# An attention sandwich on one core: the attention result is packed channel-major through DRAM instead of transposed on TensorE, and the first and last turns get lists of their own

## The chip, the cores and the metric

One core of one Trainium2 chip. The metric is the time of one execution on the device in microseconds. Inputs are float32, and every matrix product is held close to float32 accuracy: each operand is split into a high and a low part in a reduced float32 format (`..._hi`, `..._lo`), and three products (hi·hi, hi·lo, lo·hi) are added.

## What is computed

The input x has 32 batches of 512 tokens with 256 channels. The mask lets a block of 128 tokens see itself and every block whose number is a multiple of 24; with four blocks that is block 0.

```python
allowed = (bi[:, None] == bi[None, :]) | is_global[:, None] | is_global[None, :]   # bi: block of a token
def attn(x):                       # 16 heads of 16 channels
    q, k, v = split(x @ w_qkv.T + b_qkv)
    scores = einsum('bhqd,bhkd->bhqk', q / 4, k) + mask
    return einsum('bhqk,bhkd->bhqd', softmax(scores), v) ... @ w_out.T + b_out
def ffn(h):
    return relu(h @ W1 + b1) @ W2 + b2           # 256 -> 1024 -> 256
x = x + layernorm(attn(layernorm(x)))
x = x + layernorm(ffn(layernorm(x)))
```

## The kernel before

**Jobs and lists.** The work of a batch is cut into jobs, and each of the five instruction streams (TensorE, ScalarE, VectorE, GpSimd, and SP, which issues nearly all DMAs) has a list `ORDER[engine]` of jobs for one turn of the loop. A job is (name, number, batch offset); turn i does it for batch i + offset, so the stages of up to six batches overlap. An engine works through its list strictly in order, and waits by semaphore where a job needs another engine's result. In the first and last turns the same lists run, with the jobs of batches that do not exist left out (`steps`, `there`). TensorE's stream is unrolled over all turns; the others loop.

**The jobs of one batch.** `load_xa`, `ln1_stats/mean/rstd/apply` (normalization, in halves), `x1` (16 transposes on TensorE), `x1_hi`/`x1_lo` (ScalarE and VectorE read the accumulators), `qk` 0 to 3 and `v` 0, 1 (products), `qk_hi`/`qk_lo`, and `load_stack` 0 to 7: six DMAs each that stack the parts of q and k of two heads in the tile `stack`. `scores_max` 0 to 19 compute scores once, `reduce` takes row maxima from the accumulators, `max_t`, `copy_max`, `store_row`, `load_row` bring the negated maxima as one more row into `stack`; `scores` 0 to 19 compute the scores again with the maximum subtracted, `exp` writes `probs`. `pv` n multiplies the probabilities of four heads by `values`, in which each head has its 16 channels and a column of ones, so that row 16 of each head's 32 result rows is the denominator. After this:

- `read_o` n (ScalarE, L535): accumulator to `o_t`, 128 rows (4 heads x 32) by 512 tokens.
- `o_t` n (TensorE, L452 to L454): eight small transposes to token-major. Four a batch.
- `normal_o` n (VectorE, L643 to L657): reciprocal of the denominators, two multiplications into `o_n`.
- `o2` (TensorE, L449 to L451): 16 transposes of `o_n` back to channel-major; `o2_hi`, `o2_lo` (L543, L625) read the accumulators.
- `op` 0, 1: output projection; `op_out`, `lny_*`, `x1_add` (residual), `x1_keep`, `ln2_*`, `x2` (transposes), `x2_hi/lo`, `f1` 0 to 7, `relu`, `h_lo` (GpSimd), `f2` 0 to 3, `f2_out`, `lnf_*`, `final_add`, `store`.

**Accumulators.** There are four pairs of banks (`RING`). The fourth entry of a TensorE job names its pair; the job before it on that pair must have been read out first (`unit_before`, `free`).

**Loading the weights.** SP loads all weights at the start; ScalarE writes their high parts and VectorE their low parts, `w_qkv` first, the rest after `qk` 1 of batch 0 (`split_first`, `split_rest`). GpSimd's memsets of `stack` and `values` (`set_ones`) follow `ln1_rstd` 1 of batch 0.

Of the kernel before, what the change touches and what calls it, by code (L numbers as in the profile page):

```python
# [20 lines left out]

ORDER = {
    "PE": [
        ("scores_max", 17, -2, 1), ("qk", 1, -1, 2), ("scores", 6, -2, 0), ("pv", 0, -2, 3),
        ("scores", 7, -2, 0), ("f1", 4, -4, 2), ("scores", 8, -2, 3), ("f1", 6, -4, 1), ("scores", 9, -2, 0),
        ("f1", 5, -4, 2), ("o_t", 0, -2, 3), ("scores_max", 18, -2, 0), ("f1", 7, -4, 1),
        ("scores_max", 19, -2, 3), ("qk", 2, -1, 0), ("max_t", 3, -2, 3), ("scores_max", 0, -1, 2),
        ("qk", 3, -1, 0), ("scores", 10, -2, 3), ("scores_max", 1, -1, 2), ("pv", 1, -2, 1),
        ("scores", 11, -2, 3), ("scores_max", 2, -1, 2), ("scores", 12, -2, 1), ("o_t", 1, -2, 0),
        ("scores_max", 3, -1, 3), ("scores", 13, -2, 2), ("scores_max", 4, -1, 1), ("f2", 2, -4, 0),  # L30
        ("scores_max", 5, -1, 3), ("scores", 14, -2, 2), ("scores", 15, -2, 1), ("f2", 3, -4, 0),
        ("scores", 16, -2, 2), ("pv", 2, -2, 3), ("max_t", 0, -1, 1), ("scores", 17, -2, 0),
        ("scores_max", 6, -1, 2), ("scores", 18, -2, 3), ("o_t", 2, -2, 1), ("scores", 19, -2, 0),
        ("scores_max", 7, -1, 2), ("scores_max", 8, -1, 1), ("scores_max", 9, -1, 3), ("pv", 3, -2, 0),
        ("scores", 0, -1, 2), ("v", 0, -1, 1), ("x2", 0, -3, 3), ("o_t", 3, -2, 0), ("scores", 1, -1, 2),
        ("v", 1, -1, 1), ("o2", 0, -2, 0), ("scores", 2, -1, 2), ("f1", 0, -3, 3), ("scores_max", 10, -1, 1),
        ("f1", 2, -3, 2), ("f1", 1, -3, 3), ("scores_max", 11, -1, 0), ("f1", 3, -3, 2),
        ("scores_max", 12, -1, 1), ("op", 0, -2, 0), ("max_t", 1, -1, 3), ("scores_max", 13, -1, 1),
        ("scores_max", 14, -1, 3), ("op", 1, -2, 0), ("x1", 0, 0, 1), ("scores", 3, -1, 2), ("f2", 0, -3, 3),
        ("scores", 4, -1, 2), ("scores_max", 15, -1, 0), ("scores_max", 16, -1, 1), ("f2", 1, -3, 3),  # L40
        ("qk", 0, 0, 2), ("scores", 5, -1, 0), ("max_t", 2, -1, 3),
    ],
    "ACT": [
# [753 lines left out]
```

## Time and profile before

| | |
|---|---|
| three runs | 2062.49, 2060.56, 2061.07 us; median 2061.07 |
| the profiled execution | 2061.84 us, of it 2060.0 from the first to the last instruction |
| TensorE busy | 1938.2 us, 94% |
| VectorE / ScalarE / GpSimd busy | 1536.7 / 1408.6 / 722.8 us |
| DMA | 160.61 MB, 132817 packets, mean 78 GB/s |
| mean granted TensorE clock | 0.977 |

Busy time is the time in which at least one instruction of the engine runs. The matmuls overlap one another, so a group's own durations add up to more than it costs; the distance from one group's start to the next is what it costs. PE is TensorE, PEld its weight loads, DVE VectorE, ACT ScalarE, POOL GpSimd, SPq the issuing of DMAs by SP. L377 is line 377 of the kernel.

### The profile page before, as it was taken

The page shows a single profiled execution, that of the slowest core. Times are in us where ns is not written, and L with a number is a line of the kernel's source. Part 1 is how long each engine was busy: PE and PEld are TensorE (multiplying, and loading weights), DVE is VectorE, ACT ScalarE, POOL GpSimd, SP SyncE. Part 2 cuts the span into 40 slices and gives each one's busy share as a digit, 9 for nine tenths or more (in the row PEclk, how much of TensorE's full clock was granted, in tenths as well). Part 3 has the DMA queues.
Part 4 walks back from the last instruction along what each step waited for, and adds up shares of the span by engine and source line. Part 5 has one row for each costly group of instructions (what it writes and reads, how often), then busy time and mean ns, then how long its engine had stood idle before and what let it go on. Part 6 is the DMA issues. An engine that isn't in the chain of part 4 may idle for free. (4 is left out here: it accounts for less than half of the span.)

```text
span 2060.0 us, 70899 instructions
## 1 busy us (share of the span) xinstructions
PE 1938.2 (94%) x27904; PEld 1588.0 (77%) x27904; DVE 1536.7 (75%) x2916; ACT 1408.6 (68%) x2341; POOL 722.8 (35%) x905
## 2 busy tenths in 40 slices
PE   3879999999999999999999999999999999999985
PEld 2557887788888778888877888787788878778765
DVE  6577777777787777778777787877778787777631
ACT  2446677777777777777777776777777677777653
POOL 2013333333333333333333333333433334343343
PEclk8789999999999999999999999999999999999998
DMA  4343343334334333433433343343334334333200
GB/s 124 71 84 73 76 90 68 80 80 93 78 81 91 68 79 81 92 78 82 91 67 77 84 90 79 80 91 66 79 84 88 79 82 89 68 80 76 54 27 16
DMA packets 132817, 160.61 MB, mean 78 GB/s; under 512 B 29408, under 2 KB 82400, under 8 KB 132576
## 3 DMA queue, kind: packets, MB, share of 16 engines
q1 hardware_dynamic: 132048, 156.29, 35.8%
q8 instruction: 222, 3.64, 0.8%
q10 hardware_dynamic: 528, 0.52, 0.1%
q14 instruction: 19, 0.16, 0.0%
HBM read 38.21 MB, written 17.83 MB: 27 GB/s over the span
## 5 line engine op out<-in xcount | busy, mean ns | idle before, releaser
L613 DVE TENSOR_REDUCE max_bias<-p_pair 128x4 f32<-128x1024 f32 (+1 forms) x640 | 761.4, 1215 | 104.1 <-PE p_pair L363 87.9
L530 ACT ACTIVATE probs<-p_pair 128x1024 f32<-128x1024 f32 x640 | 638.8, 1027 | 246.4 <-PE p_pair L363 134.9
L746 POOL TENSOR_TENSOR h_lo<-h_f,h_hi 128x512 fp32r<-128x512 f32 x256 | 329.8, 1288 | 477.5 <-ACT h_hi L562 477.4
L366 PE MATMUL p_pair<-stack 49*128 49x256 f32 (+1 forms) x3072 | 352.3, 314 | 36.3 <-ACT probs L530 15.0
L562 ACT ACTIVATE h_f<-p_pair,b_s 128x256 f32<-128x256 f32 x512 | 247.9, 484 | 119.3 <-PE p_pair L393 119.3
L366 PEld LDWEIGHTS p_pair<-stack 49*128 49x128 f32 (+1 forms) x3072 | 241.3, 191 | 111.6 <-ACT probs L530 46.8
L393 PE MATMUL p_pair<-x_hi,w_hi 64*128 64x256 f32 (+1 forms) x2560 | 302.6, 308 | 13.0 <-DVE x_lo L625 5.5
L393 PE MATMUL p_pair<-w_hi,h_hi 64*128 64x256 f32 x2048 | 286.7, 277 | 10.0 <-POOL h_lo L746 7.4
L393 PE MATMUL p_pair<-x_hi,w_lo 64*128 64x256 f32 (+1 forms) x2560 | 295.9, 302 | 0.0
L393 PE MATMUL p_pair<-x_lo,w_hi 64*128 64x256 f32 (+1 forms) x2560 | 295.7, 302 | 0.0
L393 PE MATMUL p_pair<-w_lo,h_hi 64*128 64x256 f32 x2048 | 284.1, 274 | 0.0
L393 PE MATMUL p_pair<-w_hi,h_lo 64*128 64x256 f32 x2048 | 283.9, 274 | 0.0
L562 ACT ACTIVATE h_hi<-p_pair,b_s 128x256 fp32r<-128x256 f32 x512 | 249.1, 486 | 0.0
L363 PE MATMUL p_pair<-stack 49*128 49x512 f32 (+1 forms) x1024 | 220.2, 433 | 19.6 <-DMA stack<-qk 7.3
L393 PEld LDWEIGHTS p_pair<-x_hi,w_hi 64*128 64x128 f32 x2560 | 213.5, 187 | 24.1 <-DVE max_bias L613 13.0
L393 PEld LDWEIGHTS p_pair<-x_hi,w_lo 64*128 64x128 f32 x2560 | 215.8, 186 | 11.7
L393 PEld LDWEIGHTS p_pair<-x_lo,w_hi 64*128 64x128 f32 x2560 | 215.5, 186 | 11.7
L393 PEld LDWEIGHTS p_pair<-w_hi,h_hi 64*128 64x128 f32 x2048 | 192.9, 185 | 15.1 <-POOL h_lo L746 6.0
L432 PEld LDWEIGHTS p_pair<-probs,values 128*32 128x32 f32 x3072 | 106.3, 112 | 120.5 <-issue 81.0
L393 PEld LDWEIGHTS p_pair<-w_lo,h_hi 64*128 64x128 f32 x2048 | 193.1, 185 | 2.8
L432 PE MATMUL p_pair<-probs,values 128*32 128x256 f32 x3072 | 194.2, 385 | 0.0
L393 PEld LDWEIGHTS p_pair<-w_hi,h_lo 64*128 64x128 f32 x2048 | 192.7, 185 | 0.0
(77 smaller groups left out, 2815.6 us busy)
## 6 DMA issues: line engine op xcount, KB each, us to landing
stack<-qk SPq DMA_DIRECT2D x1536, 64.0 KB, 2.3
xr<-x SPq DMA_DIRECT2D x32, 512.0 KB, 4.0
out<-yf SPq DMA_DIRECT2D x64, 256.0 KB, 2.2
xa<-x SPq DMA_DIRECT2D x31, 512.0 KB, 4.5
shift_rows<-max_t SPq DMA_DIRECT2D x128, 8.0 KB, 1.3
stack<-shift_rows SPq DMA_DIRECT2D x128, 8.0 KB
probs<-w SPq DMA_DIRECT2D x2, 512.0 KB, 4.9
probs<-w_qkv_t SPq DMA_DIRECT2D x2, 384.0 KB, 5.2
```

Of the source, the lines that this page charges most:

```text
L363: last = nc.tensor.matmul(dst[:, j, :], stack[r, stationary, at, 0:P], stack[r, moving, at, :], start=True, stop=True)
L366: last = nc.tensor.matmul(dst[:, j, col:col + HALF].rearrange("p (a n) -> p a n", a=2), stack[r, stationary, at, kb * P:(kb + 1) * P], two ...
L393: last = nc.tensor.matmul(dst[:, u, cols], stationary(r), moving(r), start=part == 0 and at == 0 and m == 0, stop=part == 1 and m == adden ...
L432: last = nc.tensor.matmul(two(o, kb), v, probs[:, prob_slot(n, c), j, col:col + HALF] .rearrange("p (a n) -> p a n", a=2), start=False, st ...
L530: nc.scalar.activation(probs[:, prob_slot(quad, c), :, :], banks("scores", n)[:, :, :], ACT.Exp, scale=SCALE).then_inc(exp_done, 1)
L562: last = nc.scalar.activation(dst, banks("f1", n)[:, n % 2, u * HALF:(u + 1) * HALF], ACT.Relu, bias=b1_s[:, m:m + 1])
L613: nc.vector.tensor_reduce(dst, src, axis=AX.X, op=ALU.max, negate=True).then_inc(red_done, 1)
L746: nc.gpsimd.tensor_tensor(h_parts[1][:, m:m + 2, :], h_f[:, n % 2, :, :], h_parts[0][:, m:m + 2, :].bitcast(F32), ALU.subtract).then_inc(h ...
```

## The change

1. **No `o_t` and `o2` on TensorE.** `read_o` writes one of two halves of a bigger `o_t`. `store_o` (SP) issues two DMAs for each quad of heads: the four denominator rows spread over 128 partitions of `den_q`, and all 128 rows to `o_rows` in DRAM. `load_o` n brings, for eight heads, the 16 wanted rows of each back as `o_ch[:, n, :]`, 128 channels by 512 tokens, in the memory of `ya`.
2. **Reciprocals.** `inverse` n (VectorE, 128x32), `store_inv` n (to `inv_rows` in DRAM), `load_inv` n (one DMA that repeats each head's row for its 16 channels into `inv_b`). `normal_o` n multiplies `o_ch` by `inv_b`; `o2_hi` n and `o2_lo` n split the result. There are two of each a batch. `w_out` is permuted on the host to the new channel order.
3. **Lists.** `ORDER` is new for every engine; `FIRST` and `LAST` are explicit lists of the jobs before and after the full turns. There are 28 full turns on TensorE.
4. **Start.** Weights come on SP's and ScalarE's queues, each part with a semaphore of its own (`W_STAGE`); their splits are jobs in the lists, with low parts mostly on GpSimd. x of batch 0 comes in two halves. The first memset of `stack` runs at the very start, the second after `ln1_apply` of batch 0, that of `values` later.

```diff
                     wait(act, pv_mm, b, QUADS, n + 1)
-                    wait(act, mm["o_t"], b, QUADS, n)
-                    nc.scalar.activation(o_t[:, :], banks("pv", n)[:, 0, :], ACT.Copy).then_inc(ot_done, 1)
+                    for s in (den_in, o_out):
+                        wait(act, s[n % 2], b, 32, 16 * (n // 2))
+                    nc.scalar.activation(o_t[:, n % 2, :], banks("pv", n)[:, 0, :], ACT.Copy).then_inc(ot_done, 1)
...
+                elif what == "store_o":
+                    rows_free, den_free = count(sp, b, 16, 0), count(sp, b, KD, n // 2 + 1 - KD)
+                    wait(sp, ot_done, b, QUADS, n + 1)
+                    reached(sp, o_in[n // 2], rows_free)
+                    reached(sp, inv_done, den_free)
+                    heads = slice(4 * (n % 2), 4 * (n % 2) + 4)
+                    sp.dma_start(den_q[:, n // 2, n % 2, :],
+                                 o_t[HD:P:32, n % 2, :].rearrange("h (m t) -> h m t", t=DT)).then_inc(den_in[n % 2], 16)
+                    sp.dma_start(o_rows[n // 2, heads].rearrange("h c n -> (h c) n"),
+                                 o_t[:, n % 2, :]).then_inc(o_out[n % 2], 16)
+                elif what == "load_o":
...
+                    reached(sp, x1_done, added)
+                    sp.dma_start(o_ch[:, n, :], o_rows[n, :, 0:HD, :].rearrange("h c n -> c h n")).then_inc(o_in[n], 16)
+                elif what == "store_inv":
...
+                    sp.dma_start(inv_rows[n].rearrange("(j h) (m t) -> (h m) j t", j=2, t=DT),
+                                 inv_q[:, n, :, :]).then_inc(inv_out[n], 16)
+                elif what == "load_inv":
...
+                    sp.dma_start(inv_b[:, n, :],
+                                 inv_rows[n].unsqueeze(0).broadcast_to([HD, H // 2, L])).then_inc(inv_in[n], 16)
...
-                    wait(pe, ev["o_t"], b, QUADS, QUADS)
-                    last = transposed(dst, lambda r, m: o_n[r, m % KB, m // KB * P:(m // KB + 1) * P], KD * KB)
-                elif what == "o_t":
-                    wait(pe, ot_done, b, QUADS, n + 1)
-                    last = transposed(dst, lambda r, m: o_t[r, m * P:(m + 1) * P], KB)
...
+                elif what == "inverse":
+                    for j in range(2):
+                        wait(dve, den_in[j], b, 32, 16 * (n + 1))
+                    wait(dve, inv_out[n], b, 16, 0)
+                    nc.vector.reciprocal(inv_q[:, n, :, :], den_q[:, n, :, :]).then_inc(inv_done, 1)
                 elif what == "normal_o":
+                    wait(dve, inv_in[n], b, 16, 16)
+                    wait(dve, o_in[n], b, 16, 16)
+                    nc.vector.tensor_tensor(o_ch[:, n, :], o_ch[:, n, :], inv_b[:, n, :], ALU.mult).then_inc(on_done, 1)
```

A part of TensorE's new list, from the last `pv` of a batch to its `op` one turn of the loop later (offsets are against the turn):

```python
("pv", 3, -2, 0), ("scores_max", 12, -1, 1), ("scores", 0, -1, 3), ("max_t", 1, -1, 0), ("v", 0, -1, 2),
("x2", 0, -3, 3), ("x1", 0, 0, 0), ("scores", 1, -1, 1), ("v", 1, -1, 2), ("scores", 2, -1, 1),
("f1", 0, -3, 3), ("f1", 2, -3, 1), ("f1", 1, -3, 3), ("scores_max", 13, -1, 2), ("qk", 0, 0, 0),
("f1", 3, -3, 1), ("scores", 3, -1, 2), ("qk", 1, 0, 0), ("op", 0, -2, 3), ...
```

and of VectorE's, and SP's, for the same stretch:

```python
("x2_lo", 0, -4), ("inverse", 1, -3), ("v_out", 0, -2), ("normal_o", 0, -3), ("x1_lo", 0, -1),
("reduce", 13, -2), ("normal_o", 1, -3), ("o2_lo", 0, -3), ("o2_lo", 1, -3), ("qk_lo", 0, -1), ...
("store_o", 3, -3), ("load_xr", 0, -3), ("store_row", 1, -2), ("store_inv", 1, -3), ("load_xa", 0, 0),
("load_o", 1, -3), ("load_inv", 1, -3), ("load_stack", 6, -2), ...
```

## Rows read from the trace of the kernel before

**Rows 1.** Engine totals of the page: busy us (share of the span) xinstructions.
```profile
PE 1938.2 (94%) x27904; PEld 1588.0 (77%) x27904; DVE 1536.7 (75%) x2916; ACT 1408.6 (68%) x2341; POOL 722.8 (35%) x905
```

**Rows 2.** Windows: from:to, length; busy us PE, PEld, DVE, ACT, POOL; PEclk, DMA, GB/s.
```profile
1001.55:1061.67 60.12, 59.15 (x876) 48.93 (x872) 47.55 (x91) 43.73 (x74) 22.32 (x28) 1.00 0.38 82
0.00:178.00 178.00, 123.89 (x1202) 86.90 (x1204) 120.66 (x184) 72.80 (x91) 23.66 (x37) 0.81 0.40 89
178.00:1915.00 1737.00, 1705.55 (x25134) 1408.48 (x25136) 1369.12 (x2621) 1262.76 (x2106) 643.47 (x807) 1.00 0.38 81
1915.00:2060.00 145.00, 108.77 (x1575) 92.59 (x1572) 46.90 (x113) 73.05 (x147) 55.66 (x62) 0.90 0.11 31
```

**Rows 3.** Timeline of VectorE, `values`: start us, length us, engine, line, operation.
```profile
289.29 1.21 DVE L638 TENSOR_TENSOR values<-p_pair,max_bias 128x1024 f32<-128x1024 f32 x1
...
1855.52 1.21 DVE L638 TENSOR_TENSOR values<-p_pair,max_bias 128x1024 f32<-128x1024 f32 x1
```

**Rows 4.** Timeline of TensorE about the transposes of one batch.
```profile
1007.30 0.40 PE L393 MATMUL p_pair<-w_hi,x_hi 64*128 64x256 f32 x4
...
1008.72 0.66 PE L377 MATMUL p_pair<-ident,xr 64*128 64x64 f32 x16
1009.21 0.42 PE L377 MATMUL p_pair<-ident,o_t 64*128 64x64 f32 x8
1009.43 0.48 PE L363 MATMUL p_pair<-stack 49*128 49x512 f32 x2
...
1011.17 0.66 PE L377 MATMUL p_pair<-ident,o_n 64*128 64x64 f32 x16
1011.63 0.49 PE L366 MATMUL p_pair<-stack 49*128 49x256 f32 x4
```

**Rows 5.** Waits of TensorE, 200 to 1900 us: us in total, times, longest.
```profile
PE p_pair L366 <- DVE o_n L652: 5.1, 28, 0.2
```

**Rows 6.** Groups by line: busy us, mean ns of one | idle before.
```profile
L652 DVE TENSOR_TENSOR o_n<-p_pair,den 128x128 f32<-128x128 f32 x256 | 62.4, 285 | 4.4
L668 DVE TENSOR_TENSOR yf<-p_pair,b_s 128x512 f32<-128x512 f32 x64 | 43.9, 687 | 65.0 <-PE p_pair L393 49.4 <-DMA out<-yf 15.6
L625 DVE TENSOR_TENSOR o_lo<-p_pair,o_hi 128x1024 fp32r<-128x1024 f32 x32 | 38.9, 1214 | 0.8 <-ACT o_hi L543 0.8
```

**Rows 7.** Timeline of GpSimd and VectorE; line 695: ns shortest, median, longest.
```profile
1044.00 1.29 POOL L746 TENSOR_TENSOR h_lo<-h_f,h_hi 128x512 fp32r<-128x512 f32 x1 [0.17 <-ACT h_hi L562]
1044.08 1.23 DVE L695 SCALAR_TENSOR_TENSOR nmr_lny<-mv_lny,rstd_lny 128x2 f32<-128x2 f32 x1
...
L695 DVE SCALAR_TENSOR_TENSOR nmr_lny<-mv_lny,rstd_lny x64: 130/146/1271, 130.1 to 1996.8; 128x2 f32<-128x2 f32 x64
```

**Rows 8.** DMA issues of the page: count, KB each, median us to landing.
```profile
out<-yf SPq DMA_DIRECT2D x64, 256.0 KB, 2.2
xa<-x SPq DMA_DIRECT2D x31, 512.0 KB, 4.5
shift_rows<-max_t SPq DMA_DIRECT2D x128, 8.0 KB, 1.3
```

**Rows 9.** Timeline of SP's issuing of DMAs.
```profile
1001.86 0.33 SPq L332 DMA_DIRECT2D shift_rows<-max_t  x1
1004.88 0.54 SPq L336 DMA_DIRECT2D stack<-shift_rows  x1
...
1046.72 3.80 SPq L323 DMA_DIRECT2D stack<-qk  x6
```

**Rows 10.** Timeline of the start: VectorE, GpSimd, TensorE.
```profile
8.44 7.28 DVE L705 TENSOR_SCALAR xa<-xa,mv_ln,rstd_ln 128x256 f32<-128x256 f32 x2 [0.26 <-POOL rstd_ln L739]
8.47 7.10 POOL L726 MEMSET stack<- 32x4096 f32 x2
33.48 0.80 PE L363 MATMUL p_pair<-stack 48*128 48x512 f32 x2 [6.62 <-DMA stack<-qk]
```

More of the change, by code:

```diff
@@ L29 @@
[L29 to L39, printed above, removed]
@@ L89 @@
+READ = {"scores_max": 20, "scores": 20, "max_t": 4, "pv": 4, "op": 1, "x2": 1, "f1": 8, "f2": 2,
         "x1": 1, "qk": 4, "v": 1}
 PAIR_OF = {job[:2]: job[3] for job in ORDER["PE"]}
[L91 to L94 removed]
 def sandwich(nc, x, w_qkv_t, b_qk, b_v, w_out_t, b_out, w1, b1, w2, b2, ident_in, out):
@@ L228, in opens, with full_turns @@
             return what not in CROSSED or which % 2 == 0
-        def unit_before(what, which, i):
-            jobs = [job for job in ORDER["PE"] if opens(*job[:2])]
-            mine = [job[:2] for job in jobs].index((what, which))
-            for at in range(mine - 1, -4 * len(jobs), -1):
-                name, n, off, pair = jobs[at % len(jobs)]
-                b = i + at // len(jobs) + off
-                if pair == PAIR_OF[what, which] and there(b):
-                    return name, n, b
-            return None
+        def full_turns(engine):
+            offsets = [job[2] for job in ORDER[engine]]
+            return TURNS[0] - min(offsets), NB - max(offsets) - TURNS[1]
@@ L241, in reads, with steps @@
         def reads(name, n):
             return (n // 2 + 1) * READ[name] // PRODUCTS[name] if name in CROSSED else n + 1
-        def steps(eng, jobs, job, early=None, unrolled=False):
-            def turn(i):
-                todo = [(what, n, i + off) for what, n, off, *_ in jobs if there(i + off)]
+        def steps(eng, engine, job, early=None):
+            start, stop = full_turns(engine)
+            for what, n, b in FIRST[engine]:
+                job(what, n, b)
+            for what, n, off in ORDER[engine]:
+                job(what, n, start + off)
+            with eng.Fori(start + 1, stop) as i:
+                todo = [(what, n, i + off) for what, n, off in ORDER[engine]]
@@ L251, in turn @@
                 for at, (what, n, b) in enumerate(todo):
-                    if early and not isinstance(i, int):
+                    if early:
                         early(what, todo[at + 1:])
-                    job(what, n, b, i)
-            if unrolled:
-                for i in range(-AHEAD, NB + BEHIND):
-                    turn(i)
-                return
-            for i in range(-AHEAD, LOOP_FROM):
-                turn(i)
-            with eng.Fori(LOOP_FROM, NB - AHEAD) as i:
-                turn(i)
@@ L264, in steps @@
-            for i in range(NB - AHEAD, NB + BEHIND):
-                turn(i)
+                    job(what, n, b)
+            for what, n, b in LAST[engine]:
+                job(what, n, NB + b)
         def two(ap, kb):
```

537 lines of the change are left out of this document (391 added, 146 removed), and 12 rows, old and new, of tables (FIRST, LAST, ORDER).

## The prediction

> **What bounds the kernel now.** I read the engine totals first: TensorE is busy 1938.2 us of 2060.0, far more than VectorE at 75% or ScalarE at 68% [rows 1]. Then the windows [rows 2]: one turn of the loop (60.12 us) has TensorE busy for 59.15 us at full granted clock, VectorE for 47.55, ScalarE for 43.73. So a steady turn is TensorE's own work plus about 1 us of gaps. Next the length of a turn: the addition that writes `values` runs once for each batch, at 289.29 us for one and at 1855.52 us 26 batches later [rows 3], so 60.24 us a turn on average. Last, the ends. Between 178 and 1915 us lie 28.8 turns with 1705.55 us busy, 59.15 a turn. Thirty-two turns' work at that rate is 1893 us, so the other 167 us of the span are the idle time (54.1 us before 178 us, 31.5 in the middle, 36.2 after 1915 us [rows 2]) and about 45 us of slow clock (0.81 before 178 us, 0.90 after 1915 us). Those two ends are 90 us idle; the loop is nearly full.
>
> **The change, part by part**, against the profiled execution (2061.84 us, 2060.0 of it the span; the median of the runs shown is 2061.07, 0.8 lower, which I take off at the end).
>
> *Transposes removed from TensorE.* One `o_t` unit starts at 1009.21 us and the next unit at 1009.43: 0.22 us. The `o2` unit starts at 1011.17 us and its follower at 1011.63: 0.46 us [rows 4]. A batch has four and one: 4 x 0.22 + 0.46 = 1.34 us, all on the engine that bounds. 32 x 1.34 = **-43 us**. These steps are pipelined and I take starts, not durations, since durations overlap.
>
> *Waits that go with them.* An accumulator pair holding `o_t` is given free by `normal_o` on VectorE. In the steady part 28 turns wait there for 5.1 us in all [rows 5]. With five of 65 units gone from the ring, these go: **-5 us**. The rest of the gaps (mainly on `exp`) I leave as they are. Bounds: nothing, or as much again.
>
> *VectorE.* Out: eight multiplications of 285 ns and one `o2_lo` of 1214 ns, 3.5 us. In: two `normal_o` and two `o2_lo` on 128x512, each taken as the 687 ns of the 128x512 addition, 2.7 us [rows 6]. Four small reciprocals against two of twice the size I take as equal. So about 0.8 us less of 47.55. ScalarE: `o2_hi` becomes two of 128x512 instead of one of 128x1024, which by VectorE's 2 x 0.69 against 1.21 is at most +0.3 us of 43.73. Both are covered by 12 us or more of idle time a turn, so they cost nothing, and nothing is gained.
>
> *The two new SBUF-to-SBUF operations.* `normal_o` and `o2_lo` read two SBUF tensors, where before one input was an accumulator. The 128x2 `nmr_lny` of 1044.08 us lasts 1.23 us against a median of 146 ns, and GpSimd's `h_lo` runs from 1044.00 to 1045.29 beside it [rows 7]. So such an operation may be held by up to one `h_lo`, 1.1 us. In the new lists ScalarE issues `relu` 0 and 1 around the two `o2_hi`, so `h_lo` will run just when `normal_o` and `o2_lo` do. On VectorE that is at most 4 x 1.1 = 4.4 us a turn of 12 idle, no cost by itself; it counts in the chain below. (The Trainium skill, SBUF — State Buffer, section SBUF: two separate sides, says that an operation of VectorE with two SBUF inputs and a GpSimd operation that reads SBUF exclude each other for the whole instruction. The trace agrees, by the row of 1.23 us; by this rule the change would carry a delay that the removed form, with an accumulator as input, did not have.)
>
> *The round trip through DRAM.* After `pv` 3 the chain to `op` of that batch is: `read_o` (128x512, taken as 0.7 us like the addition of that size [rows 6]), `store_o` (denominators), `inverse`, `store_inv`, `load_inv` (queued behind `load_xa` and `load_o`), `normal_o` 1, `o2_hi`, `o2_lo` 1. Three transfers: the 8 KB store of the row maxima lands after a median of 1.3 us, but the load that waits for it once started 3.0 us after it (1001.86, 1004.88); loads from DRAM of 512 KB take 4.5 us, the 256 KB store 2.2 [rows 8, 9]. Low end, with the reciprocal as one of the 285 ns multiplications: 0.7 + 1.3 + 0.3 + 1.3 + 2.2 + 0.7 + 0.6 + 0.7 and 0.8 for eight handovers = 8.6 us. High end: 1.8 (behind one `lnf_apply`) + 3.0 + 0.3 + 3.0 + 4.5 + 0.7 + 0.6 + 0.7 + 0.8, plus two holds of 1.1 and about 2 us of queueing on VectorE and SP = 19.6 us. I take 13.9: small transfers of 2.0, the broadcast at 3, one hold and 2 us of queueing.
> The cover: between `pv` 3 and `op` 0 in the new TensorE list stand `v` twice and `f1` four times (24 matmuls of 256 columns each; `v` takes 1007.30 to 1008.72, 1.42 us), `qk` twice (half as many of 512 columns, so about the same), `x2` and `x1` (0.49, 1008.72 to 1009.21), six score units at about 0.3 and a `max_t` of 0.1 [rows 4]. 8 x 1.42 + 2 x 0.49 + 6 x 0.3 + 0.1 = 14.2 us. So the trip is covered by a hair: +0.2 us a turn x 28 = **+6 us**, from 0 to (19.6 - 14.2) x 28 = 151. If it is late, `op` on TensorE waits, and behind it the whole in-order list. VectorE waits too, at `inverse` 1 and `normal_o`: behind them stand `v_out`, `x1_lo` and `reduce` 13, whose results TensorE needs only for `scores_max` 13 and `qk` 0, later in the turn.
>
> *SP's queue.* Six stack copies are issued in 3.80 us, 0.63 each; other DMAs take from 0.33 us [rows 8, 9]. Before: 48 x 0.63 + 12 x 0.45 (between 0.33 and 0.54) = 36 us of a turn. Added: eight DMAs of `store_o` and six of the others, 14 at 0.33 to 0.63, 5 to 9 us. SP is then busy 41 to 45 us of 59: covered, unless its in-order waits (each new DMA has one) delay a stack copy. `load_stack` 4 of the next batch may go after `scores` 14, and `scores_max` 10 then needs it some 14 units and 8 to 9 us on; it takes 3.8 + 2.3 = 6.1 us. I count it at nothing, bound +1 us a turn. *Bytes.* 82 GB/s x 60.12 us is 4.9 MB a turn at 0.38 of the DMA engines [rows 2]; 2.1 MB are added (four stores and four loads of 256 KB), so about 0.55. Cover, nothing.
>
> *First turns.* Today VectorE's second `ln1_apply` lasts 7.28 us beside GpSimd's two memsets of 7.10 us at 8.44 us, and the first matmul waits for it [rows 10]. The new list does one memset before x has landed, and the other after `ln1` is applied: -6.5 us. `qk` 2 and 3 now run while the first stack copies are on their way (TensorE waits for these until 33.48 us [rows 10]): up to -2.6 us. From 58 to 178 us TensorE is idle another 20 us; own orders may win half: -10. Together **-18 us**, bounds -7 (the memset alone) and -35.
>
> *Last turns.* 36.2 us idle after 1915 us [rows 2]. The new list puts `f1` and `f2` of batch 30 (4 x 1.42 + 2 x 2.8 = 11 us) between the last `pv` and the last `op`, which covers most of the new trip; the same chain from `op` over two normalizations to `f1` stays. **-5 us**, bounds -15 and +8.
>
> Sum: -43 - 5 + 6 - 18 - 5 = **-65 us**, 2061.84 - 65 = 1996.8, and 0.8 less against the median: **1996 us**. The turn would be 60.24 - 1.34 - 0.2 + 0.2 = 58.9 us.
>
> **Rivals.**
> *A. The trip is late each turn by 1 to 2 us.* For it: the high end above, and the new hold by `h_lo`. Against it: I found 13.9 against 14.2. Price 1.2 x 28 = +34 us: about 2030.
> *B. Slower than before.* The same wait, larger: TensorE stops in front of `op` every turn until the broadcast reciprocals have landed. To cancel 65 + 6 us it must cost 71 / 28 = 2.5 us a turn, that is a trip of 16.7 us. Part of it could be the clock: it is 1.00 (2.4 GHz) in the full middle and falls to a mean of 0.81 and 0.90 at the ends, where TensorE has gaps [rows 2]. With a trip of 18 us, 3.8 us a turn: 1990 + 106 = 2096. For it: three serial DMAs on one queue that carries 40% more bytes. Against it: the middle values reach only 13.9.
> *C. SP is the late one.* Its waits push stack copies past their use: bound +1 us a turn, 2024.
> *D. More than forecast.* All gaps of TensorE but half go (31.5 us in the middle, -14 more) and the first turns give 25: about 1970.
> *E. It does not do what it says*: the units are gone, but TensorE's freed time turns fully into waits for `exp` and `reduce`, and only the first turns gain. VectorE and ScalarE are idle 12 and 16 us a turn, which speaks against it; 2061 - 5, within 0.2%.
>
> **How the numbers follow.** Forecast (1980 to 2012) 0.54, A 0.17, C 0.06, D 0.10, E 0.03, B 0.10. The range leaves out B and the far part of D: 1970 to 2045. A measurement of this kernel can tell about 0.2% from no change. Faster by more than that (under 2057): forecast, A, C, D = 0.87; the same 0.03; slower 0.10.
>
> **What would show it.** A turn of 58.9 us between two `values` additions; TensorE's busy time of 57.8 a turn; its 1536 transposes of `o_t` and `o_n` gone; no wait of TensorE's `op` matmuls on `o2_lo` over 0.5 us (A and B: 1.2 to 4 us there); first `scores_max` at about 25 us; SP's issues 41 to 45 us a turn; DMA share near 0.55. Wrong would be: a turn over 60 us; VectorE waiting at `normal_o` for a DMA for longer than its idle time; a granted clock under 1.00 in the middle.

## The result and the profile after

The changed kernel takes 2124.58 us (median; 2119.76 to 2132.95) against 2060.82 us for the kernel before: ratio 1.031, 95% interval 1.029 to 1.034. It is 64 us slower, where I had forecast 65 us faster. In all that follows a ratio is to runs of the kernel before on the same chip. The profiled execution took 2119.76 us, with a span of 2117.9 us.

The page's engine totals of the changed kernel (busy us, share of the span, instructions) answer to [rows 1]:

```profile
PE 1926.8 (91%) x26368; PEld 1568.7 (74%) x26368; DVE 1545.5 (73%) x2689; ACT 1407.5 (66%) x2375; POOL 751.4 (35%) x910
```

The 1536 transposes are gone (27904 - 26368), yet TensorE's busy time fell by only 11 us. Windows of the changed kernel, one full turn and the middle, in the columns of [rows 2]:

```profile
1035.28:1096.85 61.57, 58.26 (x828) 47.91 (x826) 48.71 (x86) 43.70 (x74) 23.01 (x28) 1.00 0.49 114
300.00:1800.00 1500.00, 1417.94 (x19930) 1165.30 (x19932) 1163.12 (x2026) 1055.95 (x1790) 553.93 (x674) 0.99 0.49 113
```

and the same middle of the kernel before:

```profile
300.00:1800.00 1500.00, 1472.79 (x21712) 1216.51 (x21708) 1183.94 (x2271) 1087.83 (x1811) 554.34 (x698) 1.00 0.39 81
```

In a turn TensorE is busy 58.26 us (forecast 57.8, before 59.15), but the turn is 61.57 us (forecast 58.9). Idle time in the middle went from 27 to 82 us of 1500, and the mean granted clock fell below 1.00, which I had named as a sign of being wrong. The `values` additions of batches 4 and 30 give the average turn, as in [rows 3]:

```profile
290.12 1.16 DVE L906 TENSOR_TENSOR values<-p_pair,max_bias 128x1024 f32<-128x1024 f32 x1
...
1904.97 1.23 DVE L906 TENSOR_TENSOR values<-p_pair,max_bias 128x1024 f32<-128x1024 f32 x1
```

(1904.97 - 290.12) / 26 = 62.11 us against 60.24. What TensorE waited for in the middle: first the changed kernel, then the one before (each row: who waited, for whom, us in total, times, longest):

```profile
PE p_pair L658 <- DVE o_lo L884: 41.4, 25, 2.0
PE p_pair L631 <- DVE max_bias L876: 17.4, 48, 0.6
PE p_pair L631 <- ACT probs L796: 9.9, 24, 0.4
PE p_pair L628 <- ACT probs L796: 4.2, 23, 0.2
```

The kernel before:

```profile
PE p_pair L366 <- ACT probs L530: 8.0, 50, 0.2
PE p_pair L366 <- DVE o_n L652: 4.5, 25, 0.2
PE p_pair L366 <- DVE max_t L617: 4.2, 24, 0.2
PE p_pair L393 <- DVE max_bias L613: 2.8, 15, 0.2
```

Per turn (25 in the window): 1.66 us at `op` for `o2_lo`, and 1.26 us in `scores` and `scores_max` for the evictions of `exp` and `reduce`, where the kernel before had 0.6 (for `exp`, `copy_max` and `reduce`) and, at `normal_o`, 0.18. One `op` of the changed kernel, by the timelines of VectorE, GpSimd and TensorE:

```profile
1042.22 1.27 DVE L919 TENSOR_TENSOR ya<-ya,inv_b 128x512 f32<-128x512 f32 x1 [0.89 <-DMA inv_b<-inv_rows]
1043.41 2.38 DVE L884 TENSOR_TENSOR o_lo<-ya,o_hi 128x512 fp32r<-128x512 f32 x2
...
1041.65 1.29 POOL L1019 TENSOR_TENSOR h_lo<-h_f,h_hi 128x512 fp32r<-128x512 f32 x1 [12.21 <-ACT h_hi L833]
1043.11 1.53 POOL L1019 TENSOR_TENSOR h_lo<-h_f,h_hi 128x512 fp32r<-128x512 f32 x1 [0.17 <-ACT h_hi L833]
...
1045.94 0.50 PE L658 MATMUL p_pair<-w_hi,o_hi 64*128 64x256 f32 x4 [1.43 <-DVE o_lo L884]
```

The trip took 1029.71 (`pv` 3 ends) to 1045.94 = 16.2 us, of which it had 14.8 us of cover. The way there has two parts that are late. The second `normal_o` starts when the broadcast reciprocals land: VectorE stands idle for 0.89 us for this transfer here, and for 37.9 us in 24 turns of the middle. Then `normal_o` takes 1.27 us and the pair `o2_lo` 2.38; alone they take 0.69 and 1.47 (see *h_lo1_after* below). Both began beside an `h_lo` of GpSimd and ended after it: `h_lo` ends at 1042.94 and `normal_o` 0.55 us later.

The last thing is the pace of TensorE itself. The timeline of `f2` of the kernel before (each row is two matmuls):

```profile
992.25 0.28 PE L393 MATMUL p_pair<-w_hi,h_hi 64*128 64x256 f32 x2
...
993.63 0.28 PE L393 MATMUL p_pair<-w_hi,h_hi 64*128 64x256 f32 x2
```

and of the changed one:

```profile
1049.23 0.28 PE L658 MATMUL p_pair<-w_hi,h_hi 64*128 64x256 f32 x2
...
1050.67 0.28 PE L658 MATMUL p_pair<-w_hi,h_hi 64*128 64x256 f32 x2
```

Twelve rows apart in both: 1.38 / 24 = 57.5 ns from start to start before, 1.44 / 24 = 60.0 ns after, for the same instruction. The recorded duration (0.28 us a pair) doesn't show it.

### The profile page after: what moved, and what is told of

It is laid out like the page before. It is cut to its first block and busy times, and to the rows that moved or that the text cites. A ratio compares the mean times of both kernels' runs of the same rounds, so it can differ in the third digit from the quotient of the medians.

```text
span 2117.9 us, 68614 instructions
## 1 busy us (share of the span) xinstructions
PE 1926.8 (91%) x26368; PEld 1568.7 (74%) x26368; DVE 1545.5 (73%) x2689; ACT 1407.5 (66%) x2375; POOL 751.4 (35%) x910
## 5 line engine op out<-in xcount | busy, mean ns | idle before, releaser
L876 DVE TENSOR_REDUCE max_bias<-p_pair 128x4 f32<-128x1024 f32 (+1 forms) x640 | 770.8, 1217 | 203.7 <-PE p_pair L631 164.1
L1019 POOL TENSOR_TENSOR h_lo<-h_f,h_hi 128x512 fp32r<-128x512 f32 x256 | 346.5, 1354 | 549.9 <-ACT h_hi L833 549.9
L631 PE MATMUL p_pair<-stack 49*128 49x256 f32 (+1 forms) x3072 | 295.4, 295 | 48.9 <-DVE max_bias L876 25.7
L658 PE MATMUL p_pair<-w_hi,h_hi 64*128 64x256 f32 x2048 | 298.2, 285 | 11.1 <-POOL h_lo L1019 6.0
L631 PEld LDWEIGHTS p_pair<-stack 49*128 49x128 f32 (+1 forms) x3072 | 231.8, 189 | 100.6 <-DVE max_bias L876 48.9
L658 PE MATMUL p_pair<-w_lo,h_hi 64*128 64x256 f32 x2048 | 294.3, 282 | 0.0
L658 PE MATMUL p_pair<-w_hi,h_lo 64*128 64x256 f32 x2048 | 294.1, 281 | 0.0
L802 ACT ACTIVATE o_t<-p_pair 128x512 f32<-128x512 f32 x128 | 76.7, 599 | 268.8 <-PE p_pair L697 268.8
L628 PE MATMUL p_pair<-stack 48*128 48x512 f32 (+1 forms) x1024 | 209.8, 451 | 27.4 <-DMA stack<-qk 14.6
L658 PEld LDWEIGHTS p_pair<-w_hi,h_hi 64*128 64x128 f32 x2048 | 199.9, 189 | 15.2 <-POOL h_lo L1019 5.7
```

What stands on the lines that cost most here:

```text
L628: last = nc.tensor.matmul(dst[:, j, :], stack[r, stationary, at, 0:P], stack[r, moving, at, :], start=True, stop=True)
L631: last = nc.tensor.matmul(dst[:, j, col:col + HALF].rearrange("p (a n) -> p a n", a=2), stack[r, stationary, at, kb * P:(kb + 1) * P], two ...
L658: last = nc.tensor.matmul(dst[:, u, cols], stationary(r), moving(r), start=part == 0 and at == 0 and m == 0, stop=part == 1 and m == adden ...
L802: nc.scalar.activation(o_t[:, n % 2, :], banks("pv", n)[:, 0, :], ACT.Copy).then_inc(ot_done, 1)
L876: nc.vector.tensor_reduce(dst, src, axis=AX.X, op=ALU.max, negate=True).then_inc(red_done, 1)
L1019: nc.gpsimd.tensor_tensor(h_parts[1][:, m:m + 2, :], h_f[:, n % 2, :, :], h_parts[0][:, m:m + 2, :].bitcast(F32), ALU.subtract).then_inc(h ...
```

## The experiments

**The trip through DRAM.** Three kernels that were to shorten it; the second keeps the first one's edit, the third starts again from the changed kernel. *xa_late*: the load of `xa` goes behind the trip's last load.

```
-("store_inv", 1, -3), ("load_xa", 0, 0), ("load_o", 1, -3), ("load_inv", 1, -3),
+("store_inv", 1, -3), ("load_o", 1, -3), ("load_inv", 1, -3), ("load_xa", 0, 0),
```

> The changed kernel with one edit: in SP's loop list the 512 KB load of x stands behind load_inv 1 instead of ahead of load_o 1. Theory 1 (each turn TensorE waits in front of op for the trip through DRAM, 1.66 us on average): the reciprocals and o have the DMA engines to themselves, load_inv goes out and lands 1 to 1.5 us sooner, the wait in front of op falls to about 0.5 us, the turn from 62.1 to about 61, the kernel to 2085 to 2100 us. Theory 2 (the added bytes slow TensorE's operand reads and everything else, wherever they are): no change, 2124 +- 5. Theory 3 (the new order in the ring of accumulators costs the time, op's wait is only where it shows): the wait in front of op falls but turns up again at the matmuls behind it, 2115 to 2125.

2121.41 us, ratio 1.029 (1.027 to 1.031). The wait at `op` fell from 41.4 to 30.2 us in 25 turns. *inv_first* also puts the reciprocal ahead of `x2_lo`:

```
-("x2_lo", 0, -4), ("inverse", 1, -3),
+("inverse", 1, -3), ("x2_lo", 0, -4),
```

> As the one before, and in VectorE's loop list inverse 1 stands ahead of x2_lo. There inverse 1 starts at 1035.02 us although VectorE was idle and waiting for x2_hi before; it can start about 1.5 us sooner. Theory 1: the wait in front of op is gone, the turn about 60.3 us, 2065 to 2080 us. Theory 2: no change from 2124. Theory 3: 2110 to 2125, the time back at other waits for reduce and exp.

2120.32 us, ratio 1.030 (1.028 to 1.032); wait 26.2 us. In both the wait fell and the time hardly moved: TensorE ran at half clock for 65 us between 300 and 1800 us, against 27 in the changed kernel. *no_recip_trip* loads the broadcast from a constant and doesn't wait for `store_inv` to land (SP still issues `store_inv`, `load_xa` and `load_o` first, in its order):

```
-wait(sp, inv_out[n], b, 16, 16)
-... inv_rows[n].unsqueeze(0).broadcast_to([HD, H // 2, L])
+... w1[0:H // 2, 0:L].unsqueeze(0).broadcast_to([HD, H // 2, L])
```

> The changed kernel, but load_inv brings a constant block of w1 instead of the reciprocals and does not wait for store_inv; all transfers are made as before. The attention result is scaled by wrong factors, so the output is not the reference's. Theory 1: the trip is shorter by inverse, one store and its landing, about 5 us, the wait in front of op is gone altogether, the turn is what is left, 60.0 to 60.5 us, 2055 to 2070. Theory 2: still about 2110 to 2120. Theory 3: 2105 to 2120.

2113.8 us, ratio 1.025 (1.023 to 1.027), and the wait at `op` was 41.5 us: not a microsecond less. This doesn't acquit the last transfer, because the edit didn't make it earlier. `load_inv` was issued 7.8 us after the end of `pv` 3 (mean of the turns) in place of 8.1, and took a median of 4.3 us to land in place of 3.8. VectorE waited for it as before; in *op_early* below, whose list edits do make it earlier, hardly at all. The rows are those of the changed kernel, *no_recip_trip* and *op_early*, 300 to 1800 us:

```profile
DVE ya L919 <- DMA inv_b<-inv_rows: 37.9, 24, 2.9
DVE ya L918 <- DMA inv_b<-w: 42.3, 24, 3.1
DVE ya L919 <- DMA inv_b<-inv_rows: 1.9, 3, 1.1
```

In most turns of both kernels TensorE's wait was one of two values, 1.43 to 1.46 or 1.98 us, however late the transfer was, and `o2_lo` was again held by an `h_lo`. That points at GpSimd as a second cause.

**The bytes.** *before_traffic* adds twelve DMAs a turn to the kernel before.

```
+("extra", 0, -2), ... ("extra", 7, -2)     # on SP: 4 stores of 256 KB with 4 small ones, 4 loads
```

> The kernel before, with twelve DMAs a turn added on SP that nobody waits for: four stores of 256 KB and four small stores to scratch rows in DRAM, four loads of 256 KB from w1 into a tile that is not read. Theory 1: TensorE's list is untouched, within 5 us of 2061. Theory 2: the rate of f2's matmuls falls from 57 to 60 ns each as in the changed kernel, and the turn grows by 1 to 2 us, 2090 to 2120 us. Theory 3: as theory 1.

2296.69 us, ratio 1.115 (span 2297.7 us, 103 GB/s). Too blunt: SP issues in order, so the extras delayed `store`, and TensorE waited for VectorE's `f2_out`, which waited for it (203.7 us on VectorE). But the matmuls of `f2` still came every 57.3 ns under 103 GB/s, so it is not the bytes that slow them.

**The place of the tiles.** The tiles ahead of `o2_hi` changed size. `o2`, `ya`, `xr`, `x2`, `h` and `yf` began 64 bytes past a multiple of 128 in every partition; now they begin on one, as the weights do. *pad64* puts 64 unused bytes into the changed kernel, *before_shift* into the one before:

```
+pad = sb("pad", [P, 16])      # pad64: ahead of o2_t; before_shift: behind den
```

> The changed kernel with one unused tile of 64 bytes per partition placed ahead of o2_hi. In the kernel before, the tiles from o2 on (o2, ya, xr, x2, h_f, h, yf) begin 64 bytes past a multiple of 128; the changed sizes of the tiles ahead of them put them on multiples of 128, and the pad puts them back. Theory of the layout (the slower cadence of the f2 matmuls, 60.0 ns against 57.1, comes from where h lies): cadence back at 57 ns, TensorE busy about 1.0 us less in a turn, turn 61.3 -> about 60.3, time about 2090 us (2080 to 2105). Theory of the bytes (the new transfers slow the operand reads) and theory of the order: cadence stays at 60 ns and the time at 2120 +- 5.

> The kernel before with the same 64 bytes added behind den, so that its tiles from o_n on begin on multiples of 128, as in the changed kernel. Nothing else differs. Theory of the layout: the f2 matmuls go from 57 to 60 ns and the time rises by 0.6 to 1.1 us in each of 32 turns, to about 2080 to 2095 us. Any other theory of the cadence: 2061 +- 3.

*before_shift*: 2080.14 us, ratio 1.008 (1.006 to 1.010), its turn 60.63 us in place of 60.10, the waits nearly unchanged. Nothing but addresses was changed: those of all tiles from `o_n` on. *pad64*: 2115.89 us, ratio 1.024 (1.022 to 1.027); its `f2`:

```profile
1050.05 0.28 PE L659 MATMUL p_pair<-w_hi,h_hi 64*128 64x256 f32 x2
...
1051.41 0.28 PE L659 MATMUL p_pair<-w_hi,h_hi 64*128 64x256 f32 x2
```

1.36 / 24 = 56.7 ns. So the place costs 0.5 us a turn in the kernel before. In *pad64* the time came down by 9 us (0.7% by the ratios), less than forecast. TensorE's busy time in a full-clock turn fell by 0.6 us, but the turn itself only from 61.41 to 61.27 us, since the waits took the rest, and half clock took more of the middle (65 us against 27). Nor is the pace mended in every unit: 33 of 96 undisturbed units of `f2` still came at 59 ns, 55 at 56.5. *ones_early_pads*, below, shows that the distance to a multiple of 128 isn't the whole rule.

**The exclusion.** *h_lo_after* starts `h_lo` 0, *h_lo1_after* only `h_lo` 1, behind both `o2_lo`:

```
 wait(pool, ev["f1"], b, 8, n + 1)
+if n == 0 and not isinstance(b, int):      # n == 1 in h_lo1_after
+    wait(pool, ev["o2"], b + 1, KD, KD)
```

> The changed kernel, but GpSimd starts the four h_lo of a turn only when both o2_lo of VectorE are through. Theory of the exclusion (a VectorE instruction with two SBUF inputs and GpSimd's h_lo hold each other up, which is what makes TensorE wait 1.43 or 1.98 us at op): o2_lo 2.38 -> about 1.2 us, the wait of op falls from 1.66 to under 0.8 us a turn, the turn by 0.8 to 1.2 unless relu 2, which waits for h_lo 0, makes the exps late; time about 2085 to 2100 us. Theory of the trip through DRAM (the last transfer sets op): the wait stays at about 1.5 us, time 2120 or more.

> The changed kernel, but GpSimd starts h_lo 1 (not h_lo 0) only when both o2_lo are through, so relu 2, which waits for h_lo 0, is not held up; the orders of the other engines are as changed. Theory of the exclusion: normal_o 1 is still held by h_lo 0, the two o2_lo take about 1.2 us in place of 2.4, the wait of op falls from 1.66 to 0.3 to 0.6 us, the turn by 1.0 to 1.3 us, and if the low-clock stretches of the middle come from the long waits at op they go as well: 2075 to 2095 us. Theory of the trip through DRAM: op is still late by 1.0 us or more.

*h_lo_after*: 2122.95 us, ratio 1.031 (1.026 to 1.036). The wait at `op` fell from 41.4 to 16.8 us, and a new one took its place, as the expectation had feared:

```profile
PE p_pair L658 <- ACT h_hi L833: 20.4, 23, 0.9
...
PE p_pair L658 <- DVE o_lo L884: 16.8, 18, 1.4
```

*h_lo1_after* has no such wait: 2115.14 us, ratio 1.026 (1.022 to 1.030). Its timeline, VectorE and then GpSimd:

```profile
1165.27 0.72 DVE L919 TENSOR_TENSOR ya<-ya,inv_b 128x512 f32<-128x512 f32 x1 [1.45 <-DMA inv_b<-inv_rows]
1165.91 1.47 DVE L884 TENSOR_TENSOR o_lo<-ya,o_hi 128x512 fp32r<-128x512 f32 x2
...
1167.46 1.29 POOL L1021 TENSOR_TENSOR h_lo<-h_f,h_hi 128x512 fp32r<-128x512 f32 x1 [2.02 <-DVE o_lo L884]
```

`o2_lo` 1.47 us in place of 2.38: held before, free now. The wait at `op` is 22.0 us in 25 turns. In 18 turns `normal_o` lasts its plain 0.69 us, and the wait, 0.53 to 1.5 us, grows with the time that VectorE stood idle for the transfer (42.5 us in all); in six `normal_o` is still held, and the wait is 0.53. So most of what is left is the transfer. The Trainium skill (SBUF — State Buffer, section SBUF: two separate sides) gives the exclusion of such an operation and one of GpSimd as a rule; the runs agree, 2.38 against 1.47 us.

**Both at once.** *op_early* is *h_lo1_after* with the two list edits of *inv_first*; *op_early_pad* has the 64 bytes too.

> The same wait of h_lo 1, and the trip shortened as in two runs before (load_xa behind the last load of the trip; the second reciprocal ahead of x2_lo). Both theories: wait of op under 0.4 us. Clean turns 60.85 - 0.97 + 0.2 = about 60.0 us. If the long waits bring the stretches of low clock, fewer than 10 us of them stay between 300 and 1800 us (65 us in the run without the wait), and the time is 2065 to 2085; if the stretches come from something else they stay and it is 2090 or more.

> The same with the 64 unused bytes ahead of o2_hi. Theory of the layout: another 0.4 to 0.6 us a turn less, clean turns 59.4 to 59.6 us, 0.5 under the kernel before (60.1), time 2045 to 2065 us: it holds the transposes' gain that the changed kernel lost. If the low clock stays: 2080.

*op_early*: 2100.36 us, ratio 1.017 (1.016 to 1.019). The wait at `op` was gone (1.2 us in all the middle). With the list edits alone it was 26.2 us, with the hold alone lifted 22.0: the transfer and the hold were both late, and neither mend is enough by itself. The one full-clock turn took 59.82 us, near the 60.0 expected. But the others took 61.4 us, nearly all with a piece of 3.41 us (once 6.83) in which TensorE ran at half clock; 82 us of them between 300 and 1800. My theory that the long wait at `op` brought them fell. *op_early_pad*: 2079.46 us, ratio 1.007 (1.005 to 1.008). Its windows, one turn without and one with a piece:

```profile
720.39:779.61 59.22, 57.38 (x828) 47.48 (x824) 48.34 (x85) 43.56 (x74) 22.94 (x28) 1.00 0.51 119
1145.24:1206.17 60.93, 59.12 (x827) 47.57 (x824) 48.22 (x84) 43.55 (x74) 22.91 (x28) 0.97 0.50 116
```

59.22 us is 0.9 under the kernel before: here is the gain, and a piece of half clock costs 1.7 us, more than all of it. Where in the turn? Windows of *op_early*, 3 us each:

```profile
1196.00:1199.00 3.00, 2.53 (x32) 1.47 (x24) 3.00 (x7) 2.23 (x3) 0.96 (x3) 1.00 0.56 100
1199.00:1202.00 3.00, 2.46 (x18) 1.24 (x20) 3.00 (x7) 3.00 (x5) 0.89 (x2) 0.77 0.39 68
1202.00:1205.00 3.00, 3.00 (x32) 0.95 (x24) 2.58 (x4) 0.00 (x0) 1.27 (x1) 0.66 0.57 185
```

Right behind a cluster of short waits in the run of `scores` and `scores_max` (VectorE and ScalarE both at 3.00 of 3.00), the clock falls from 2.4 to 1.2 GHz.

**Gaps or work?** *light_evict* takes the evictions of that run down to half their columns; *exp_twice* does the opposite to the kernel before.

```
+few = slice(0, HALF) if n in (15, 16, 17, 18) ...       # light_evict: exp; reduce 7 to 10 likewise
+if n == 17 and not isinstance(b, int):                  # exp_twice: into a tile nobody reads
+    nc.scalar.activation(again[:, :, :], banks("scores", n)[:, :, :], ACT.Exp, scale=SCALE)
```

> op_early_pad with less work in one place: in the turns of the loop the exps 15 to 18 and the reductions 7 to 10 take half their columns (part of the softmax and of the row maxima is left out, so the time is not that of the whole computation). TensorE's work is unchanged. In op_early_pad TensorE waits there four to five times in 4 us (1.2 to 1.8 us a turn), and a piece of half clock of 3.41 us follows in most turns. Theory of the gaps (a stretch with many waits brings the half clock): waits of that place under 0.4 us, half clock under 10 us in 300 to 1800, turns of 58.3 to 58.8 us, time 2015 to 2035. Theory of the work (the half clock comes from what TensorE computes or from the transfers, whatever the waits): half clock stays at 60 to 90 us, turns about 60.3, time 2060.

> The kernel before, with exp 17 of each turn of the loop run twice (the first time into a tile nobody reads), so that ScalarE is 1.0 us late where scores and scores_max follow each other. Theory of the gaps: TensorE waits 0.7 to 1.0 us more there, and pieces of half clock appear in the middle, of which the kernel before has none: turn 61.0 from the wait alone, 62 to 63 with a piece in most turns; time 2090 to 2150. Theory of the work or of the transfers: no half clock in the middle, time 2085 to 2092.

*exp_twice*: 2095.46 us, ratio 1.016 (1.014 to 1.017), with ten pieces of half clock (34 us) in the middle, where the kernel before has none. One turn without and one with a piece, then the windows about the piece:

```profile
658.21:719.23 61.02, 58.86 (x880) 48.93 (x874) 47.67 (x93) 44.60 (x74) 22.29 (x28) 1.00 0.39 81
719.23:781.32 62.09, 60.20 (x880) 49.23 (x874) 47.65 (x92) 44.71 (x74) 22.27 (x28) 0.97 0.38 79
...
768.00:771.00 3.00, 2.20 (x36) 1.26 (x28) 2.03 (x8) 2.20 (x3) 1.17 (x4) 1.00 0.01 3
771.00:774.00 3.00, 2.51 (x20) 1.51 (x24) 2.49 (x6) 3.00 (x5) 0.57 (x1) 0.68 0.25 44
```

TensorE's instructions and the bytes are the same: one late eviction a turn is enough for the half clock. Each of the ten pieces begins 0.4 to 0.9 us behind a wait of 1.08 us for `exp`; the other turns have the same wait and no piece. (The Trainium skill, TensorE: Matmul & The Clock Gate, section A second HAM failure mode: psum-queue depth-cycling, tells of a kernel whose clock swings because TensorE idles briefly between groups of matmuls as it cycles through PSUM banks. This run shows the like: 34 us at half clock, with no wait over 1.1 us.) *light_evict* was not the counterpart I meant: 2073.84 us, ratio 1.006, half clock 55 us. The waits on `exp` went, but TensorE, now early, waited up to 1.6 us at once for stack copies and up to 1.2 us for reductions:

```profile
PE p_pair L629 <- DMA stack<-qk: 19.9, 18, 1.6
...
PE p_pair L629 <- DVE max_bias L880: 7.3, 7, 1.2
```

It doesn't refute the theory of the gaps and doesn't add to it.

*f2_later* moved `f2` 3 of *op_early_pad* behind `scores` 15, to break the run up:

```
-("scores_max", 4, -1, 1), ("f2", 3, -4, 0), ("scores_max", 5, -1, 1), ("scores_max", 6, -1, 3), ("scores", 15, -2, 2),
+("scores_max", 4, -1, 1), ("scores_max", 5, -1, 3), ("scores_max", 6, -1, 1), ("scores", 15, -2, 2), ("f2", 3, -4, 0),
```

> op_early_pad with f2 3 (2.9 us of matmuls that need no eviction in between) moved behind scores_max 5, 6 and scores 15, with the PSUM pairs of these units exchanged to match, so that the run of scores and scores_max behind it is shorter. All theories: the waits move. If each part of the run stays under the rate of the evictions, waits of 1.3 us fall to about 0.8, the half clock goes in part, and the time is 2050 to 2070; if scores_max 6 waits for the reduction 4 instead, 2075 to 2095.

2103.4 us, ratio 1.019 (1.017 to 1.021): the waits moved to `exp` (44 us in the middle) and grew. An order found for one rate of evictions isn't mended by one swap.

**Half of the largest term by itself.** A batch has 32 small matmuls in its four `o_t` and 16 in its `o2`. The next run leaves out 24 of these 48, and leaves `o2` whole; by the starts that the prediction took, 3/4 x 4 x 0.22 = 0.66 us a turn, half of its 1.34 (the expectation says three quarters, about 1.0, which counts `o2` in). The first try, *few_transposes*, ran the kernel before unchanged (its condition never held; 2063.09 against 2063.3 us, which shows how well two series agree). *few_transposes_2*:

```
-last = transposed(dst, lambda r, m: o_t[r, m * P:(m + 1) * P], KB)
+last = transposed(dst, lambda r, m: o_t[r, m * P:(m + 1) * P], 1 if 1 < b < NB - 1 else KB)
```

> The kernel before, in which each o_t of batches 2 to 30 transposes one block of columns in place of four, 2 matmuls in place of 8 (the rest of o is left out, so the time is not that of the whole computation). It prices three quarters of my largest term, 1.34 us a turn: about 1.0 us. Forecast as in the sum: turn 60.1 to 59.1 us, time 2030 to 2036, with no half clock. Rival: the transposes filled time in which TensorE would have waited for ScalarE's and VectorE's evictions: the waits of scores and scores_max grow by as much as the transposes give, turn 59.7 to 60.1, time 2048 to 2061; or half clock appears where the waits have grown, 2060 or more.

2083.63 us, ratio **1.009** (1.008 to 1.011): leaving out three quarters of the `o_t` transposes, and nothing else of TensorE's work, makes the kernel before 20 us slower. Its windows, a turn at full clock and one with a piece of half clock:

```profile
1025.70:1085.74 60.04, 58.65 (x850) 48.27 (x850) 46.66 (x92) 43.73 (x73) 22.32 (x28) 1.00 0.39 82
1392.20:1453.73 61.53, 60.16 (x850) 48.53 (x850) 46.67 (x92) 43.84 (x73) 22.31 (x28) 0.97 0.40 83
```

and its waits:

```profile
PE p_pair L366 <- ACT probs L530: 17.2, 49, 0.4
PE p_pair L428 <- ACT h_hi L562: 3.8, 23, 0.2
```

TensorE's busy time fell by 0.5 us a turn, the wait for `exp` rose from 8.0 to 17.2 us in the middle, one of 3.8 us for `h_hi` came up, and a full-clock turn is 60.03 us against 60.10. So the transposes had filled time in which TensorE would have waited. Fifteen pieces of half clock, 51 us, came up where there had been none, most of them just behind a wait of 0.35 us and one of 0.18. That it is the longer waits that brought them, and not the smaller amount of work, is argued from *exp_twice*; no run separates the two in this place.

**The ends.** *plain_last* runs the changed kernel's last turns from the steady list, as before:

```
+LAST = {engine: [(what, n, i + off) for i in ... for what, n, off, *_ in jobs if i + off < 0] ...}
```

> The changed kernel, but its last turns run the list of the steady turn to its end, as the kernel before does, in place of their own lists. My term for the last turns was -5 us (-15 to +8). If their own lists gain what I forecast, this is 5 us slower than the changed kernel, 2125 to 2135; if the last turns lost 6.7 us because of their lists, 2110 to 2118; within 3 us of 2121: the lists are worth nothing and the last turns lose by the longer way through DRAM alone.

2135.68 us, ratio 1.033 (1.031 to 1.036). From the last `values` to the end: 144.5 us before (2060.0 - 1915.53), 151.2 after (2117.9 - 1966.66), 157.2 here (2135.5 - 1978.32). So by these traces the own lists gain 6.0 us, and the steady list with the new path costs 12.7; in those 12.7 TensorE waits 5.0 us for `o2_lo`, where the kernel before waits 1.0 for `o_n`. The medians don't show the gain clear of noise: the intervals of the two ratios, 1.031 to 1.036 and 1.029 to 1.034, overlap. *ones_early* takes the first turns' main edit alone to the kernel before:

```
+stack_ones(0)                       # at the very start
-pool.wait_ge(rstd_done["ln1"], 2)   # then both halves
+pool.wait_ge(norm_done["ln1"], 2)   # then the second half
```

> The kernel before with one part of the change alone: the first half of the ones of stack is set at the very start, the second half behind the layer norm's apply, as the changed kernel does, in place of both between the rstd and the apply. By the first-turn term of my sum the first transposes start 5 to 7 us earlier, and if the start sets the end one for one the time is about 2055 us; if the first turns hold the gain back at the loads of the weights or at the low clock, within 2 us of 2061.

2057.41 us, ratio 0.9975 (0.9956 to 0.9993). *ones_early_pads* adds 64 bytes ahead of `x1_hi` and behind `den`:

> The kernel before with the early first half of the ones, and two unused tiles of 64 bytes: one ahead of x1_hi, so that x1, qk and stack too begin 64 bytes past a multiple of 128 while the weights begin on one, and one behind den, so that the later tiles stay where they were. Theory of the layout as the runs so far bear it (matmuls of a tile that begins like the weights come every 59 to 60 ns, others every 57): the 112 matmuls of v and qk in a turn gain about 2 ns each or 4 for those of 512 columns, 0.2 to 0.3 us a turn, turn 60.1 -> 59.8, time 2048 to 2053 us. If only the place of h matters: 2055 to 2059, as ones_early, about 5 under the kernel before.

2059.5 us, ratio 0.9979 (0.9967 to 0.9991), its turns 60.1 us at the least, 60.24 in the median. That is no gain, yet the pace of the matmuls did change. Those with `x2` as the moving tile and weights as the stationary one (`f1`) came faster, about 57 ns in place of 59 in most units. Those of `f2` came slower: in 69 of 98 units every 59 ns, in 29 every 56.5, where all 100 units of the kernel before have 56.5. Two units of one turn, twelve rows apart each:

```profile
987.79 0.28 PE L395 MATMUL p_pair<-w_hi,h_hi 64*128 64x256 f32 x2
...
989.16 0.28 PE L395 MATMUL p_pair<-w_hi,h_hi 64*128 64x256 f32 x2
...
991.23 0.28 PE L395 MATMUL p_pair<-w_hi,h_hi 64*128 64x256 f32 x2
...
992.65 0.28 PE L395 MATMUL p_pair<-w_hi,h_hi 64*128 64x256 f32 x2
```

1.37 / 24 = 57.1 ns and 1.42 / 24 = 59.2 ns. The two pads move `h` by 128 bytes, so it still begins 64 bytes past a multiple of 128, and the rule as I expected it fails here. *ones_early* and *ones_early_pads* are the versions that beat both kernels, by 0.2%, with none of the change's new data path.

## Why the prediction was wrong, point by point

Three steps failed: the -43 for the transposes was taken as time saved, the trip's wait was taken as 0.2 us a turn, and the waits for evictions and the clock were left as they are.

**Transposes, -43: sized fairly, but not time saved one for one.** In *op_early_pad* a full-clock turn has 57.38 us busy against 59.15. But I priced it as if every freed microsecond ended the turn earlier. With half of them taken out by themselves, 0.66 us by their starts, a full-clock turn became 0.07 us shorter, and the kernel 20 us slower by the half clock. With the whole change and its other losses mended, a full-clock turn is 0.9 us shorter, and the kernel with its half clock still 0.7% slower than before. My rival E (freed time turns into waits for `exp` and `reduce`) had part of the mechanism; I gave it 0.03 because VectorE and ScalarE are idle 12 and 16 us a turn. That average says nothing about the stretches where both are at 3.00 of 3.00. That the clock would fall for it no rival had.

**Waits on the accumulators, -5: failed.** They went (0.18 us a turn), and those for `exp` and `reduce` rose by 0.66 us, from 0.6 to 1.26. I had left them "as they are" with the new order of TensorE unexamined.

**The trip, +6: mechanism right, sized wrong, and the largest error in a turn.** The cover was 14.8 us (I had 14.2), the trip 16.2 (I had 13.9), and the wait 1.66 us a turn: rival A's 1 to 2 us, 49.7 us over the 32 batches. Two things set it together. The broadcast reciprocals landed late: `inverse` started 5.3 us after `pv` 3 ended, where my middle values give about 3, and `load_inv` was issued 3.2 us after `store_inv` and took 3.8 to land, where I had 2.0 and 3. And `h_lo` held `normal_o` or `o2_lo`, often both. I had put one hold of 1.1 us into the middle value and two into the upper bound. The mend of either left 1.05 and 0.9 us a turn of the wait; that of both left 0.05.

**Layout: missing.** No term stood for the pace of instructions that the change doesn't touch. 0.5 us a turn by *before_shift*, 16.5 us by the medians; from *op_early* to *op_early_pad* 21 us.

**Clock: named, not priced.** "A granted clock under 1.00 in the middle" was in my list of signs, and in rival B only for waits of 3 us and more. In these runs it came behind clusters of waits of 0.2 to 0.4 us (five of the six stretches in the middle of the changed kernel, the sixth behind a wait of 1.98 us at `op`), and in *exp_twice* behind one wait of 1.1 us. A piece costs about 1.1 us (*exp_twice*) to 1.7 us (*op_early_pad*).

The turn, then: forecast 58.9; +1.46 wait at `op` over the 0.2 in the sum; +0.66 evictions, and the 0.2 I had taken off for `normal_o` was right; +0.5 layout; together 61.5, as the full-clock turn of 61.57 shows. The average of 62.11 has 0.5 more, from half clock (27 us between 300 and 1800). Over the kernel, the span is 123 us over the forecast one: 26 turns at 62.11 in place of 58.9 make 83 of it, the first 290 us some 19 and the last turns 12.

**SP, VectorE, ScalarE, bytes: right.** DMA share 0.49 (forecast 0.55); VectorE busy 48.71 us a turn (I had 46.8, the holds are in it), ScalarE 43.70; SP's issuing took 44.6 us a turn (forecast 41 to 45), a DMA of the trip mostly 0.38 to 0.59 us. Rival C did not come true: waits on stack copies are 2.0 us in the middle.

**First turns, -18: only the start was right.** The first transposes start at 8.55 us and the first `scores_max` at 26.23 (forecast about 25), 7 us earlier. But by batch 4 nothing is left: `values` at 290.12 against 289.29. The lead was 8 us at batch 2 (160.95 against 169.12), and TensorE was busy for 232.1 us of the first 290, against 233.9. In *ones_early* the steady list keeps the lead (`values` at 281.14, the time 6 us shorter by the medians), so the changed kernel lost it in batches 2 to 4: its time between these `values` is 129.2 us against 120.2.

**Last turns, -5: +6.7 in the traces.** The own lists gave 6.0 by one pair of traces, near the forecast, if it is more than noise. But the steady list with the new path cost 12.7, and I had let `f1` and `f2` of batch 30 cover all of the trip there. The waits for `o2_lo` are 2.2 us after 1915 us in the changed kernel; where the rest of the 12.7 comes from wasn't tested.

**Open.** Which of the list's differences brings the waits for `exp` and `reduce`: I tried one swap. What makes `f2` run at 56.5 or at 59 to 60 ns: on a multiple of 128 bytes no undisturbed unit had 56.5 (*before_shift* and the changed kernel); 64 bytes past one all had it in the kernel before, 55 of 96 in *pad64*, 29 of 98 in *ones_early_pads*. So the place matters, and it isn't the only thing that does. Why some turns with the same waits have a piece of half clock and others none.

## What to carry to other kernels

An operation on the bounding engine is only worth its time if nothing else would stand there: before pricing its removal, look at the stretch around it, not at the average, and ask what the engine would wait for next; one run that leaves out part of the operation answers this before anything is rebuilt. A removal that opens several short gaps can also cost the clock, which can take back more than the operation did. An experiment that removes a cause must be seen to have done so in its own trace: a load that no longer waits isn't earlier if others still stand ahead of it in the queue. When a change resizes tiles, compare the addresses of all later ones, and time a shift of 64 bytes.
